# A delta-rule layer in chunks: swapped head halves for the outputs, scan products grouped, and a new order of work on every engine

## What is computed

```
xn  = layernorm(x)
q,k,v = silu(short_conv(xn @ W.T))        # 4 taps
o   = delta rule, chunk by chunk: S' = S + k^T (u - w S);  o_i = q_i S + attn_i (u_i - w_i S)
o   = gates: p0*fir_s(v) + p1*fir_m(v) + p2*fir_l(v) + p3*o + p4*v      # FIR filters of 3, 15, 63 taps
x1  = x + layernorm(rmsnorm(o) @ Wo.T)
y   = x1 + layernorm(sigmoid(xr @ Wr.T) * (relu(xk @ Wk.T)**2 @ Wv.T))  # xr, xk: mixes of xn2 and its shift by one
```

## Time and profile before

| what | us |
|---|---|
| median of 3 runs | 636.95 (635.76 to 636.98) |
| profiled execution, span | 636.7 |
| TensorE busy | 550.6 (86%) |
| VectorE busy | 462.5 (73%) |
| GpSimd busy | 335.2 (53%) |
| ScalarE busy | 277.0 (44%) |
| chain that ended last | PE 44%, POOL 18%, issue 14%, DVE 13%, DMA 5%, SPq 3% |

### The profile page before, as it was taken

The page is one execution under the profiler, slowest core; times in us unless marked ns, Lnnn a source line. Parts: engine busy times, 40 slices in busy tenths (PEclk is TensorE's granted clock), DMA queues, the critical chain, the costliest instruction groups (busy, mean ns, idle before and its releaser), DMA issues.

```text
span 636.7 us, 24446 instructions
## 1 busy us (share of the span) xinstructions
PE 550.6 (86%) x10028; PEld 446.9 (70%) x10028; DVE 462.5 (73%) x1182; ACT 277.0 (44%) x688; POOL 335.2 (53%) x408
## 2 busy tenths in 40 slices
PE   2888848999888989799999998989888999999964
PEld 2566636666666768687778877878776878887753
DVE  3788693655695844777858878788867878888863
ACT  5788881111553533453524533453432444433421
POOL 9976104877301633458343456834469776555522
PEclk9999988999997977799979989999989999999988
DMA  9729336797045144421533241341232142322101
GB/s 288 201 73 266 114 114 166 163 223 156 18 84 100 37 88 86 73 51 26 115 65 67 52 88 31 77 86 43 59 65 47 35 101 52 67 61 53 35 16 35
DMA packets 138815, 56.98 MB, mean 89 GB/s; under 512 B 108112, under 2 KB 130512, under 8 KB 138704
## 3 DMA queue, kind: packets, MB, share of 16 engines
q1 hardware_dynamic: 138704, 55.42, 39.6%
HBM read 36.43 MB, written 18.95 MB: 87 GB/s over the span
## 4 chain that ended last, share of the span: by engine, by line
PE 44%; POOL 18%; issue 14%; DVE 13%; DMA 5%; SPq 3%; ACT 2%; POOLq 0%; DVEq 0%; ACTq 0%
PE bank L1867 7%; PE bank L1717 7%; PE bank L1638 6%; PE bank L1757 4%; POOL arena L641 4%; DVE cva L1119 3%; PE bank L1552 3%; POOL arena L588 3%; PE bank L1892 2%; DVE arena L1229 2%; POOL arena L604 2%; POOL seq L632 2%; POOL seq L543 2%; POOL seq L630 2%; PE bank L1647 1%
## 5 line engine op out<-in xcount | busy, mean ns | idle before, releaser
L641 POOL TENSOR_TENSOR arena<-arena,neg_half 128x2 f32<-128x2 f32 (+1 forms) x64 | 61.5, 961 | 124.2 <-DVE arena L1337 84.8
L1229 DVE SCALAR_TENSOR_TENSOR arena<-bank,small,arena 128x256 f32<-128x256 f32 x192 | 91.0, 481 | 22.9 <-ACT arena L883 18.1
L1203 DVE TENSOR_TENSOR seq<-bank,seq 128x384 f32<-128x384 f32 x64 | 35.2, 557 | 30.3 <-PE bank L1638 19.5
L588 POOL TENSOR_TENSOR arena<-seq,powers 128x16 f32<-128x16 f32 x16 | 46.7, 2921 | 19.0 <-DVE seq L1245 18.6
L1638 PE MATMUL bank<-arena 128*64 128x192 f32 x512 | 50.1, 338 | 4.4 <-DVE seq L1203 2.0
L1119 DVE SCALAR_TENSOR_TENSOR cva<-bank,small,cva 128x256 f32<-128x256 f32 x96 | 40.4, 477 | 15.5 <-ACT cva L760 15.3
L559 POOL TENSOR_TENSOR seq<-seq 128x256 f32<-128x256 f32 x32 | 23.3, 729 | 48.1 <-DVE seq L1203 48.1
L1638 PEld LDWEIGHTS bank<-arena 128*64 128x64 f32 x512 | 35.1, 139 | 13.8 <-issue 6.5
L1717 PE MATMUL bank<-arena,w_k 128*128 128x268 f32 x128 | 38.8, 438 | 6.8 <-DMA arena<-xnT_scratch 5.6
L1342 DVE TENSOR_SCALAR arena<-arena 128x256 f32<-128x256 f32 x64 | 28.8, 492 | 17.1 <-POOL arena L641 17.0
L883 ACT ACTIVATE arena<-bank,small 128x256 f32<-128x256 f32 x64 | 29.4, 468 | 22.5 <-PE bank L1717 22.4
(11 more groups left out here) (170 smaller groups left out, 1430.2 us busy)
## 6 DMA issues: line engine op xcount, KB each, us to landing
arena<-fl SPq DMA_DIRECT2D x32, 192.0 KB, 6.7
arena<-fms SPq DMA_DIRECT2D x32, 192.0 KB, 7.2
arena<-xnT_scratch SPq DMA_DIRECT2D x32, 134.0 KB, 2.7
gram_scratch<-arena SPq DMA_DIRECT2D x32, 128.0 KB, 2.4
arena<-v_scratch SPq DMA_DIRECT2D x32, 128.0 KB, 3.3
arena<-x SPq DMA_DIRECT2D x32, 128.0 KB, 2.9
out<-arena SPq DMA_DIRECT2D x32, 128.0 KB, 2.5
xnT_scratch<-seq SPq DMA_DIRECT2D x2, 1027.0 KB, 6.4
```

Source lines behind the costliest of these rows:

```text
L588: pool.tensor_tensor(rk, ssel[:, slot_of(n)], powers[:, :, :], ALU.pow).then_inc(s["norms"], 1)
L641: pool.tensor_tensor(dst, src, half8 if k == U else neg_half[:, 0:k], ALU.pow).then_inc(s[dst_sem], 1)
L1203: nc.vector.tensor_tensor(fprod[:, q % (2 * FPAIRS), :], bank[fir_bank(q)][:, 0:2 * ROW], fgate[:, q // (TILES // 2), :], ALU.mult).then_i ...
L1229: nc.vector.scalar_tensor_tensor(cv[:, t], ps[:, :, j:j + C], conv_w[:, 1 - t // 2, t % 2, j:j + 1], cv[:, t], ALU.mult, ALU.add).then_inc ...
```

## The change

1. Everything that belongs to the output o changes halves: even heads on partitions 64 to 127, odd heads on 0 to 63 (gates, beta, FIR sums, sums of squares, per-head constants, rows of Wo). The scan itself keeps its halves. So q S and attn u write across: input half e, output half 1 - e.
2. `scan_k` and the q S part of `scan_o` become `scan_kq`; `scan_state` and the attn u part become `scan_so`. In each, one product over all units is followed by the other.
3. `o_turn` is four 128x128 transposes of `o_n`, which `o_normed` now writes with the pair inside the batch.
4. `y_rows` writes bank 6 (chunks 0 to 7) or 1 (from 8); `ffn_k` writes bank 5 or, from chunk 8, 2.
5. `direct` reads a tile of its own, `v_o`, which `direct_in` loads with two more DMAs per chunk, in swapped halves; `values_in` no longer waits for `ov`.
6. The lists of all five engines are written anew.

```diff
+            def scan_kq(n):
...
+                pe.wait_ge(s["oT"], n)
+                pe.wait_ge(s["o1"], n)
+                if n >= 2:
+                    pe.wait_ge(s["rl"], min(n - 1, N // 2))
                 for u in range(U):
+                    for e in range(2):
+                        last = mm(bank[4][HH[e], C * u:C * u + C], kq[slot_of(n)][HH[e], u, 0, :], S[HH[e], u, :], start=True, stop=True)
                 last.then_inc(s["ks_mm"], 1)
+                for u in range(U):
+                    for e in range(2):
+                        mm(bank[5][HH[1 - e], C * u:C * u + C], kq[slot_of(n)][HH[e], u, 1, :], S[HH[e], u, :],
+                           start=(u == 0), stop=False, skip_group_check=True)
...
             def o_turn(n):
...
-                for u in range(U):
-                    for q in HH:
-                        last = mm(bank[4][q, C * u:C * u + C], o_n[q, u, :], rstack[q], start=True, stop=True)
+                by_batch = o_n.rearrange("p (b r) d -> p b (r d)", r=PAIRS)
+                for b in range(B):
+                    last = nc.tensor.transpose(bank[4][:, P * b:P * b + P], by_batch[:, b], ident)
```

More of the change, by code:

```diff
@@ L454, in lead_step @@
             def lead_step(n):
[L456 to L467, removed]
@@ L500, in tail_step @@
-            def tail_step(n):
[L502 to L515, removed]
@@ L517, in _ @@
-            for n in range(-172, 22):
+                if 2 <= n + 15 < 10:
+                    window_in(n + 15)
+                if 0 <= n + 14 < 1:
+                    rows_in(n + 14)
+                if FIRST <= n + 15 < FIRST + 4:
+                    toep_late(n + 15)
+                if 0 <= n + 12 < 8:
+                    block_in(n + 12)
+                if 0 <= n + 10 < 2:
+                    products_in(n + 10)
+                if 0 <= n + 12 < 2:
+                    diag_in(n + 12)
@@ new lines, in tail_step @@
+            def tail_step(n):
+                if 9 <= n - 4 < N:
+                    rows_in(n - 4)
+                if 10 <= n - 1 < N:
+                    diag_in(n - 1)
+                if 9 <= n - 2 < N:
+                    values_in(n - 2)
+                    direct_in(n - 2)
+                if 10 <= n - 1 < N:
+                    products_in(n - 1)
+                if 7 <= n - 6 < N:
+                    rows_out(n - 6)
+                if n - 5 >= 8 and solving(n - 5) is not None:
+                    solved_store(solving(n - 5))
+                if 10 <= n - 1 < N:
+                    solved_in(n - 1)
@@ L518, in _ @@
+            for n in range(-170, 22):
                 lead_step(n)
@@ L1503, in tail_step @@
                 if 7 <= n - 1 < N:
+                    shifted(n - 1)
                     mix(n - 1, 1, xk)
                 if 9 <= n + 1 < N:
-                    low_in(n + 1)
+                    k_sums(n + 1)
+                if 7 <= n - 1 < N:
+                    mix(n - 1, 0, xr)
+                if n >= 8 and solving(n) is not None:
+                    blocks_scaled(solving(n))
                 if 8 <= n < N:
@@ L1934, in lead_step @@
[L1934 to L1950 removed]
+                if n + 20 == -1:
+                    banks_cleared(n + 20)
@@ new lines, in lead_step @@
+                if 0 <= n + 29 < 8:
+                    proj(n + 29, 0, 0)
+                if 0 <= n + 3 < 1:
+                    off_second(n + 3)
+                if 0 <= n + 13 < 1:
+                    k_turn(n + 13)
+                if 0 <= n + 28 < 8:
+                    gram(n + 28, 0)
+                if 0 <= n + 27 < 8:
+                    sumsq(n + 27, 1)
+                if FIRST <= n + 151 < FIRST + 8:
+                    fir_tiles(n + 151, 1)
+                if 0 <= n + 12 < 1:
+                    off_first(n + 12)
@@ new lines, in lead_step @@
+                if 0 <= n + 15 < 1:
+                    low_second(n + 15)
+                if 0 <= n + 28 < 8:
+                    gram(n + 28, 1)
+            def chunk_step(n):
+                if 0 <= n < 8:
+                    y_rows(n)
+                if 8 <= n + 8 < N:
+                    gram(n + 8, 0)
+                if 1 <= n + 1 < 9:
+                    off_second(n + 1)
+                if 8 <= n + 8 < N:
+                    sumsq(n + 8, 1)
+                if 1 <= n + 1 < 9:
+                    k_turn(n + 1)
+                if 0 <= n + 1 < 8:
+                    scan_kq(n + 1)
@@ L1998, in tail_step @@
                 if 8 <= n + 1 < N:
-                    scan_o(n + 1)
+                    scan_so(n + 1)
+                if 9 <= n + 2 < N:
+                    low_second(n + 2)
                 if 7 <= n < N:
                     x_turn(n)
-                if 8 <= n + 1 < N:
-                    scan_state(n + 1)
                 if 9 <= n + 2 < N:
-                    low_second(n + 2)
+                    k_turn(n + 2)
                 if 7 <= n - 1 < N:
                     ffn_v(n - 1)
-                if 7 <= n < N:
-                    ffn_k(n)
                 if 9 <= n + 2 < N:
                     off_first(n + 2)
-                if 8 <= n + 1 < N:
-                    o_turn(n + 1)
-                if 9 <= n + 2 < N:
-                    k_turn(n + 2)
-                if 8 <= n + 1 < N:
-                    y_rows(n + 1)
-                if 9 <= n + 2 < N:
-                    off_second(n + 2)
-                if 8 <= n + 2 < N:
-                    scan_k(n + 2)
-                if 7 <= n < N:
-                    ffn_r(n)
-            for n in range(-172, 22):
+            for n in range(-170, 22):
                 lead_step(n)
```

531 lines of the change are left out of this document (252 added, 279 removed).

## The result

The changed kernel takes **620.1 us** (median of 4 runs, 617.5 to 623.2) where the kernel before takes 636.97 beside it (635.8 to 638.9): a ratio of 0.9727, 95% interval 0.9677 to 0.9777, 17 us less. The forecast was 617.5 us, faster. Run a second time, on another chip, the same kernel gave 0.976 (0.9714 to 0.9807). The profiled execution spans 618.6 us.

What follows compares the result with a forecast made beforehand. TensorE's own work per step plus its standing time, paid twice when the clock falls, was taken as the bound; 636.7 - 8 - 6 - 3 - 2 - 0.5 = 617.2, forecast 617.5 us, range 604 to 639 (own range 610 to 625).

Steps and rivals of the forecast that it cites:

- the signs that I had named for being wrong: Crossed records further apart, clean step still 24.7 us, SyncE's loads after solves ending waits, or scan starting no earlier than 245.
- Part 1: Output turn as four transposes, 0.98 to 0.49 us: 0.45 us saved a step, 7 us in 16 steps.
- Part 2: Scan products as two pairs at 2.02 us each instead of 4.18 in sum: 0.14 us a step, 2 us in all.
- rival A: Every step and the lead: work goes but waits come back, VectorE holding TensorE up; about 630 us, chance 0.24.
- Part 3: Lead before the scan: SyncE's reordered loads bring windows and first solve earlier; -6 us, bounds 0 and -9.
- Part 4: Chunk stage: TensorE's 2.8 and 2.5 us stalls go; -3 us, bounds 0 and -13 if clock drops go too.
- "Issue": Chunk stage: 6.4 us idle before L1773, read as the instruction stream running dry, which no order removes.
- the bank of y_rows, costed at nothing: Projection in bank 6 or 1 removes scan_o's and ffn_k's wait for t1; ffn_v waits instead; no time counted.
- direct_in at nothing: Two more SyncE issues a chunk, 1.24 us together; loads queued behind have over 5 us except after a solve; 0 us.
- rival B: SyncE standing behind solved_store makes loads late, engines stand and the clock falls; +31, 648 us, chance 0.10.
- Rival C: Scan groups: crossed products do not overlap, 1.9 us times 16; +30, 647 us, chance 0.04.
- Part 5: Tail and end, net of Part 1 and Part 2: -2 us in the tail, -0.5 us in the end.

Runs made afterwards that it cites:

- e1: Changed kernel with the output turn done by the 16 matmuls of before instead of transposes: 626.17 us, ratio 0.983.
- e2: Changed kernel with q S and attn u written to the half they are read from, not across: 621.2 us, ratio 0.9769.
- e7: Kernel before with the new engine lists and new banks, but old turn, old products and uncrossed heads: 626.66 us, ratio 0.9907.
- e8: Changed kernel with plain and crossed products of each scan group alternated unit by unit: 614.07 us, ratio 0.9672.
- e11: e8 with the next group's first block loads moved behind the chunk's rows in the two solved-store steps: 610.36 us, ratio 0.9612.
- the control: The changed kernel unedited, run again as base for other runs on the same chip: 618.04 us.
- e4: Changed kernel with the first solve's solved_store ahead of block_in(4) and solved_in ahead of gram_store in SyncE's lead: 616.9 us, ratio 0.970.
- e3: Kernel before with only the new lists of all five engines; old products, banks and turn, no direct_in: 639.32 us, ratio 1.0046.
- e5: Changed kernel with the projection's rows (y_rows) back in bank 5 for the chunk stage only: 624.52 us, ratio 0.9885.
- e9: Changed kernel with direct_in's loads split into four transfers a chunk instead of two, same bytes: 625.27 us, ratio 0.9839.
- e10: e9 with the next group's first block_in moved behind rows_in in the two chunk steps with a solved store: 619.82 us, ratio 0.9771.

## Why the prediction was right, and where it was not

The time and the sign are right, the split is not. By stage of the two profiles, forecast against measured: to the first scan -6 against +1.1; chunk stage -7 against -13.8; tail -5.5 against -4.2; end -1 against -1.2. Two errors of 7 us cancelled, so that the total came within 3 us of the forecast was luck. And two of the signs that I had named for being wrong came up: the scan starts at 248.28 us, later than my limit of 245, and of the four clean steps in the two profiles of the changed kernel (the third and fourth) one takes 24.26 us and the others 24.7 to 24.9, where I had 24.0 to 24.3, although TensorE's work in them did fall.

- **Part 1, o_turn.** The 0.49 us came as read from the earlier trace rows. The term was mis-sized: 0.45 us a step forecast, 0.73 measured (e1). The missing part is 0.1 us of change of shape that falls away behind it, and the turn itself, which costs 1.07 us where a 128x128 product follows, not the 0.98 of the earlier trace rows, where another 64x64 one did. Of the 0.73 us, 4.5 to 6.6 us in all reach the total (e1), so the 7 us that I took for this part are near by two errors: more work saved, and less of it felt.
- **Part 2, the pairs.** 2.02 us is right for groups uncrossed (2.01 in e2). Crossed they take 1.83. I had looked for a penalty of crossing and taken the nearest row; that crossing could be a gain was in none of my bounds. Together 1.13 us less TensorE in the clean step (24.68 to 23.55), where I had 0.6. But only part of it reaches the clock: from e7 to the changed kernel TensorE's work in the chunk stage falls from 193.6 to 187.1 us, 6.5, and the stage from 203.9 to 199.8, 4.1. The other 2.4 us are idle time of TensorE: rival A, in small. In the tail steps of 17.88 us appear in the changed kernel, in e2, e8 and e11 alike, with 15.9 to 17.7 us of TensorE in them: another engine's cycle holds those. In that of the changed kernel, 544.51 to 562.39, VectorE is busy for 15.71 us and waits twice for a power on GpSimd (view of its waits); e2, e8 and e11 have the same 1.7 us there. That this cycle is what holds the step is read from the profiles, no run took it away.

```profile
DVE arena L1350 <- POOL arena L659: 1.7, 2, 0.9
```

- **Part 3, the lead.** This step failed. The windows are on time and the solve begins 4.0 us earlier after the first gram product, not 5.8 by the absolute time near 204 that I named; then 1.8 us are lost again, from there to the first copy of u (39.2 us, before 37.4; 38.8 to 43.1 in the thirteen profiles): the store of the solved blocks waits behind four loads (226.86, before 225.58), and VectorE turns them at 235.02, behind chunk 7's sums, where it did at 232.16. The rest can't be put down to the change: the first gram product begins anywhere between 168.0 and 172.7 us in the fourteen profiles, at 169.5 in that of before and at 172.7 in that of the changed kernel, which has 171.5 in the control. From the first gram product to the first copy of u this profile has 75.5 us where before has 77.7, but the control has 77.7 too, and the thirteen have 75.1 to 79.1: no gain is shown for the lead, where I had 6 us. That the 1.8 us are due to those two places is read from the profile and was not shown by a run (e4 missed it).
- **Part 4, stalls.** -3 us forecast; order and banks together make the chunk stage 9.7 us shorter (213.6 to 203.9, e7), of which 4.8 are idle time and 4.9 the same products at a higher clock (granted 0.98 instead of 0.96). So what happened lies nearer to my upper case, clock drops going with the stalls. And two statements were false. "Issue", which I held to be out of reach of any order, falls from 9.3 us (6.4, 2.5, 0.4) to 4.3, and with the new order and the old products to 0.5 (e3) and 1.0 (e7). And the bank of y_rows, costed at nothing, is worth 8 us (e5): the wait is not one of the kernel before, but of the new order without it. I checked the new order with the new bank, not what each is worth without the other.
- **direct_in at nothing, rival B.** Wrong in its cover: "over 5 us to spare except after a solve" is true, but after a solve there is so little that 2.6 us more in the queue cost 5 us (e9), and moving 3 us out of it likely gives back 4 (e10). Rival B's mechanism is there: even in the control VectorE waits once for the load of a diagonal, 0.8 us. Its size, at the change's two loads, stays under what I could measure.
- **Rival C** fell, by its opposite. **Part 5** came near (-5.5 against -4.2).

By experiments the 17 us (on the second chip 15) are: order with banks 5.9, and the turn and the crossed groups together 9.4 (0.9907 to 0.976; the new loads of v come in with them), the turn being 4 to 7 of it (e1) and the crossing 1 to 3 (e2). Each has an uncertainty of some 4 us.

## What to carry to other kernels

When a product fills only two quarters of TensorE's array, look for another of the same shape, ready at the same time, that could fill the other two, and write them alternately; swapping which half an output lies on can be worth it for that alone. Price a change of order together with the buffers it needs: here the order alone lost. Work taken from an engine that is no longer the bound comes back as standing time, and with it the clock can fall (the tail in e8). And look at a queue's slack where it is least, behind its longest wait, not on the mean of a step.

## What was not expected of the hardware

- 64 64x64 records in 1.09 us with plain and crossed products alternating, against 2.01 in two uncrossed groups: a factor of 1.84.
- Idle times named "issue" fall on the same instruction when a kernel is run again (before L1785 at 529.9 and 529.8 us, and before L1734 at 439.1 and 439.3 us, in the two profiles of the changed kernel), but move and shrink with the order and number of instructions (0.5 us in e3's chunk stage, 9.3 before). What they are stays open.
- The stretch up to the first gram product takes 168.0 to 172.7 us in the thirteen profiles with the new lists; in it TensorE's longest wait for VectorE's product of the FIR filters goes from 1.5 us (e5) to 3.5 (the changed kernel). A single profile can't be read there to better than 4 us.
